# New orders of work for the first and last step of an attention loop, and two key tiles summed on TensorE

## The reference

```
x = x + attention0(layernorm(x))        # 16 heads of 64, no mask
    q, k, v = z @ wq @ fcq_w + fcq_b, ...          # per head
    attn    = softmax(q k^T / 8) over 1024 keys
    out     = (attn v) over all heads @ fco_w + fco_b
x = x + experts0(layernorm(x))          # 8 experts, top 2
x = x + attention1(layernorm(x))        # latent keys, rotary, causal
x = x + experts1(layernorm(x))          # 9 experts of width 512
```

## Time and profile before

| what | value |
|---|---|
| timed runs | 1471.29 us median (1468.84 to 1474.14) |
| profiled execution | 1475.02 us, span 1473.3 us |
| mean granted TensorE clock | 0.965 |
| busy over the span | PE 93%, DVE 66%, POOL 59%, ACT 55% |
| step 0 | 64.8 to 107.5 us |
| last step to the middle part | about 692 to 737.7 us |

### The profile page before, as it was taken

One profiled execution on the slowest core, in us unless ns is written; L12 is line 12 of the kernel. 1 busy time (PEld: TensorE's weight loads), 2 busy tenths in 40 slices (PEclk: granted clock), 3 DMA queues, 4 the chain that ended last, 5 costly groups with the idle time before them and its releaser, 6 DMA issues. The chain is left out here.

```text
span 1473.3 us, 18699 instructions
## 1 busy us (share of the span) xinstructions
PE 1367.5 (93%) x6354; PEld 791.1 (54%) x6354; DVE 974.1 (66%) x1675; ACT 810.0 (55%) x1236; POOL 870.9 (59%) x685
## 2 busy tenths in 40 slices
PE   7699999999999999999888876999999988999998
PEld 5345555455544555455366633454445446687776
DVE  5676767767776766666556568677666624566665
ACT  4234454454444454354354452566776666787776
POOL 0277888988888888878544405555655232344443
PEclk9699999999999999999999898999999997999999
DMA  3101111111101111000050006011111107000000
GB/s 107 33 1 59 59 59 59 44 59 59 46 28 59 58 59 45 1 16 27 15 160 1 1 1 100 16 30 30 30 22 24 30 1 273 1 1 8 8 8 8
DMA packets 32586, 60.59 MB, mean 41 GB/s; under 512 B 9499, under 2 KB 17084, under 8 KB 32348
## 3 DMA queue, kind: packets, MB, share of 16 engines
q1 hardware_dynamic: 32492, 59.40, 14.6%
HBM read 35.13 MB, written 13.89 MB: 33 GB/s over the span
## 5 line engine op out<-in xcount | busy, mean ns | idle before, releaser
L628 POOL TENSOR_TENSOR psum_k<-psum_k,prob 128x1024 f32<-128x1024 f32 x186 | 466.6, 2541 | 115.4 <-ACT prob L680 114.9
L680 ACT ACTIVATE prob<-pair 128x1024 f32<-128x1024 f32 x256 | 247.7, 1027 | 367.1 <-PE pair L934 366.9
L739 DVE TENSOR_REDUCE mx<-pair 128x2 f32<-128x1024 f32 x256 | 297.2, 1214 | 40.4 <-PE pair L865 38.5
L906 PE MATMUL pv<-prob,c_all 128*64 128x512 f32 x1024 | 251.0, 607 | 0.9 <-ACT plain L648 0.9
L1937 DVE CUSTOM_DVE_ANT_0 l_banks<-l_banks,causal 128x128 f32<-128x128 f32 (+7 forms) x256 | 189.4, 782 | 75.5 <-PE l_banks L1975 74.4
L1845 ACT ACTIVATE l_prob<-l_banks 128x1024 f32<-128x1024 f32 (+7 forms) x256 | 155.2, 654 | 111.7 <-PE l_banks L1994 111.1
L933 PE MATMUL pair<-qq,ak 128*128 128x512 f32 x512 | 210.9, 412 | 6.0 <-issue 2.8
L934 PE MATMUL pair<-q,kb 128*128 128x512 f32 x512 | 203.5, 397 | 0.0
L2153 POOL TENSOR_TENSOR silu_rest_t<-silu_t,silu_lead_t 128x512 fp32r<-128x512 f32 x74 | 96.3, 1303 | 145.9 <-ACT silu_lead_t L2350 145.9
L1899 POOL TENSOR_SCALAR_AFFINE_SELECT l_prob<-l_prob 128x128 f32<-128x128 f32 x256 | 72.3, 295 | 146.7 <-ACT l_prob L1845 145.1
L933 PEld LDWEIGHTS pair<-qq,ak 128*128 128x128 f32 x512 | 97.7, 191 | 70.4 <-issue 29.2
(11 more groups left out here) (318 smaller groups left out, 2283.0 us busy)
## 6 DMA issues: line engine op xcount, KB each, us to landing
plain<-scratch_sums SPq DMA_DIRECT2D x32, 256.0 KB
whole<-in_experts SPq DMA_DIRECT2D x12, 512.0 KB, 5.0
scratch_lead<-rounded SPq DMA_DIRECT2D x12, 512.0 KB, 2.6
scratch_rest<-rounded SPq DMA_DIRECT2D x12, 512.0 KB, 3.9
w_lead_t<-scratch_lead SPq DMA_DIRECT2D x9, 512.0 KB, 6.4
w_rest_t<-scratch_rest SPq DMA_DIRECT2D x9, 512.0 KB, 7.3
l_kk<-rounded SPq DMA_DIRECT2D x16, 256.0 KB, 4.2
l_qq<-rounded SPq DMA_DIRECT2D x16, 256.0 KB, 5.3
```

The costliest lines, as they stand in the source:

```text
L628: nc.gpsimd.tensor_tensor(total[:, h, :], total[:, h, :], prob[kt % 4][:, h, :], ALU.add).then_inc(summed, 1)
L680: nc.scalar.activation(prob[kt % 4][:, :, ts(j, BLK)], buffer("ST", at)[:, :, :], ACT.Exp, scale=D0 ** -0.5).then_inc(exp_done, 1)
L739: nc.vector.reduce_max(mx[:, x % 2, :, x // 2], buf[:, :, :], AX.X).then_inc(read, 1)
L906: ins = nc.tensor.matmul(pv[D0 * h:D0 * (h + 1), ts(j, BLK)], m.c_all[:, TT * (s // PAIRS) + kt, :], prob[kt % 4][:, h, ts(j, BLK)], start ...
```

## The change

It adds an order for step 0, changes the order of the last step, and takes key tiles 6 and 7 of the last step out of the adds on GpSimd and VectorE; TensorE takes their probabilities in as further parts of the last sums.

```
+FIRST_STEP = ("PV PV q q ST ST ST ST ST s s PV s s PV PV s s PV ST ST ST ST ST ST ST s PV s s s PV PV PV "
+              "s s s PV PV s s PV PV s s ST ST m ST ST PV PV ").split()
-LAST_STEP = ("ST ST ST ST PV PV PV PV ST ST ST ST l PV PV PV PV ST ST ST ST PV PV r PV PV ST ST ST ST n "
+LAST_STEP = ("ST ST ST ST PV PV PV PV ST ST ST ST l PV PV PV PV ST ST ST r ST PV PV n ST ST ST ST PV PV "
              "PV PV PV PV g ").split()
-TURN_AT, ROOT_AT, NORMAL_AT, LEAD_AT, EXP_AT = 6, 12, (4, 6), 12, 4
+TURN_AT, ROOT_AT, NORMAL_AT, LEAD_AT, EXP_AT = 6, 12, (4, 6), 12, 3
...
-    for kind in STEP if n + 1 < STEPS0 else LAST_STEP:
+    for kind in FIRST_STEP if n == 0 else STEP if n + 1 < STEPS0 else LAST_STEP:
...
+SUMMED_LAST = TT - 2
...
-                for kt in range(1, TT):
+                for kt in range(1, TT if n < LAST else SUMMED_LAST):
...
-                    add_last(rest[0])
+                    if rest[0] < SUMMED_LAST:
+                        add_last(rest[0])
...
-                    if rest[0] == 2:
+                    if rest[0] == TT - 1:
                         index_two(nc, m, link)
...
-                    await_sums(pe, k, TT - 1)
-                    for q in range(4):
-                        ins = nc.tensor.matmul(buf[32 * q:32 * (q + 1), 0, :], ones[:, 0:32],
-                                               psum_k[k % 2][:, q // 2, ts(q % 2, BLK)], start=True, stop=True)
+                    parts = [psum_k[k % 2]]
+                    if k == LAST:
+                        parts += [prob[kt % 4] for kt in range(SUMMED_LAST, TT)]
+                    await_sums(pe, k, SUMMED_LAST - 1 if k == LAST else TT - 1)
+                    for i, part in enumerate(parts):
+                        for q in range(4):
+                            ins = nc.tensor.matmul(buf[32 * q:32 * (q + 1), 0, :], ones[:, 0:32],
+                                                   part[:, q // 2, ts(q % 2, BLK)], start=(i == 0),
+                                                   stop=(i == len(parts) - 1))
```

## The result

The changed kernel takes 1462.57 us in the median of six runs (1460.2 to 1465.46), where the kernel before takes 1472.45 on the same chip (six runs, 1468.84 to 1475.48). The ratio is 0.9933 with a 95% interval of 0.9917 to 0.9950: about 9.9 us less (7.4 to 12.2). A second measurement of the same kernel, further down, gives 0.9942 (0.9924 to 0.9960). So the kernel is faster by 0.6 to 0.7%, where 11.2 us, 0.76%, was forecast. The profiled execution has a span of 1459.4, 13.9 under the 1473.3 of before.

The account below looks back on a forecast made before the run. TensorE was taken to set the pace, so time removed from its stream arrives at the end. Step 0's 6.6 us plus the last step's 4.7 less 0.1 gave 11.2: 1460.0 us timed, 8-in-10 range 1454.5 to 1467.

Parts of the forecast that it names:

- step 0: First loop step: its gains and losses from the new order were summed to 6.6 us gained.
- q units in front: Step 0 start: step 1's two q units fill the DMA wait; first scores 0.5 us later, 1.9 leave the later stream.
- Clock in step 0: Step 0, first scores: TensorE's clock rises earlier, near 67.8; 1.4 us gained, bounds 0 to 2.6.
- The cover of the q units: Step 0: ScalarE's and VectorE's work on q runs behind half-clock TensorE work; cost nothing, at most 1.7 us.
- The full ring behind seven score units: Step 0, middle: the ring of three tiles runs full, the third row-max unit waits for an exponential; 0.7 us lost.
- The wait at step 1: Step 0 end: more units behind the turned maxima cut the DMA wait from 1.79 to 0.3 us; 1.5 won.
- Clock in step 1: Step 1's first 16 score matmuls: full speed, 3.88 instead of 5.38 us; 1.5 gained, bounds 0 to 1.5.
- GpSimd passes it through: Start of step 1: GpSimd's lag is 6 us instead of 6.8, so step 0's gain passes at no cost.
- The last step: Last loop step: TensorE's waits go, extra sums are added; 4.7 us gained, less 0.1 for a delayed copy.
- The copy of step 14's sums: Last step: VectorE copies near 708.6 instead of 711.49, so TensorE's 1.06 us idle time goes.
- `on`: Last step: ready at 721.7, 2.3 us before TensorE's output product asks; 1.1 late if VectorE's add follows GpSimd's.
- The extra sums: Last step's end: three sets of last sums instead of one add 2.0 us, from 1.7 to 3.4.

Follow-up runs that it names:

- first_only: Changed kernel with its last step set back (old order, all adds on GpSimd and VectorE, search after the second add): 1465.92 us, ratio 0.9948.
- after_again: The changed kernel unedited, run once more as base for a comparison on one chip: 1462.49 us, ratio 0.9942.
- exp_early: Changed kernel with one extra one-column exponential on ScalarE ahead of the loop, so the table loads in idle time: 1461.43 us, ratio 0.9925.
- adds_back: Changed kernel with key tiles 6 and 7 of the last step again added by GpSimd and VectorE: 1461.28 us, ratio 0.9922.
- after: The changed kernel itself, in its first measurement and profile: 1462.57 us, ratio 0.9933.
- index_early: Changed kernel with the index search behind the second add of the last step again: 1463.71 us, ratio 0.9944.
- q_front: Changed kernel, but step 0 in the old order with only the two q units moved to the front: 1465.77 us, ratio 0.9942.
- m_sooner: Changed kernel, but step 0 in the old order with only the turn of the maxima moved ahead: 1469.37 us, ratio 0.9974.
- sums_only: Kernel before, old orders, with only the two extra parts in the last sums on TensorE: 1468.15 us, ratio 0.9970.
- last_only: Changed kernel with the old order in step 0, so only the last step is changed: 1469.53 us, ratio 0.9968.
- best: Changed kernel with all adds back on GpSimd and VectorE, index search behind the add of tile 5, and an early exponential: 1460.04 us, ratio 0.9927.

## Why the prediction was right

The mechanism held in both ends. For the last step the agreement is firm: 4.6 was forecast (4.7 less 0.1), and the traces with the old and the changed last step differ by 4.5 to 4.6 whichever two are taken. For step 0 the agreement to 0.1 is in part luck: several terms were off and balanced, and some of them change from one execution to the next.

- **q units in front.** Forecast: scores 0.5 later. They start 4.52 behind the turn instead of 3.83: 0.7; in `first_only`, where the clock rose earlier, 0.
- **Clock in step 0.** Forecast 1.4 of a bound of 2.6. All of 2.6 came in this execution: the granted clock is 1.00 from 65.00 on. The rise came 4.6 behind the turn here (60.44 to 65.0), not the 5.9 behind a start without a break that the prediction took. The term varies: with the same order the first four score matmuls were slow in `after_again` and `exp_early`, two in `adds_back`, and in `first_only` the clock rose during the q units. A rise within the first scores is also worth less than it looks, since `after`, `after_again`, `adds_back` and `index_early` all turn the next maxima at 36.27 to 36.28: what the clock gives there, the waits of the next point take.
- **The cover of the q units**, costed at nothing, was not whole. The first five score units take 5.9 (64.96 to 70.88) where 4.85 is full speed: TensorE waits 0.40 for VectorE's subtractions and 0.24 for the first exponential, together 1.1 between the starts. The second row-max unit, which was to lose nothing once q was done, comes another 0.4 late, behind an exponential. Of this 1.5, within the bound of 1.7, 0.9 is the table load, as `exp_early` shows; the other 0.6 is VectorE's subtractions, which come behind ScalarE's activations of the q units. The prediction had the half clock as their cover, and in this execution the scores ran at full clock. I had not asked where the first exponential's table load would go once four other activations stood in front of it.
- **The full ring behind seven score units**, forecast at 0.7, cost nothing: the third row-max unit behind the run starts 0.34 after the second.
- **The wait at step 1.** Forecast 0.3, measured 0.64. The work behind the turn takes 4.5 where 4.28 was summed, and the row came 5.15 behind the turn, where it had come after 4.54. That differs from one execution to the next: wherever TensorE waited for it in this case, it came 4.20 (`q_front`) to 5.15 behind the turn, and `after_again` and `index_early` show no wait at all. `m_sooner` and `q_front` show that the wait goes with the place of the turn, and that VectorE's row maxima must keep up.
- **Clock in step 1.** Forecast 1.5, measured 1.6 in this pair of traces. It is not a fixed gain: `q_front` waited 1.45 and `sums_only` 1.56 without falling, the kernel before 1.79 and `last_only` 1.91 with a fall (granted clock 0.53 and 0.58 behind it). An execution of the kernel before in which the clock does not fall has 1.6 less to give. That may be why the timed gain is 9.9 and 8.5 rather than 11.2. The scatter of 4 us behind the loop could do it as well; the timed runs carry no trace, so neither is shown.
- **GpSimd passes it through.** Right: GpSimd is 6.8 behind at the start of step 1, before and after, and from the q units of step 1 to the sums of step 14 every trace takes 591.6 to 592.2, before included.
- **The last step.** Forecast 4.6, measured 4.6. The copy of step 14's sums was expected 0.5 ahead of the scores of tile 4 and came 1.5 behind them, since both adds waited for GpSimd (6.75 for two); it cost 0.3 of waiting before the scores of tile 5. `on` had 3.4 to spare instead of 2.3. The extra sums cost 1.7, the lower bound, not 2.0. These two balanced.
- **What the prediction gave no share.** It counted order and sums as one, so it missed that either alone ends the wait for `on`, and that with the order in place the sums on TensorE cost 0.6 more than they bring (`adds_back`).

## What to carry over

Where one engine streams without a pause in the steady part of a loop, look at its first and last turn: work that needs no transfer belongs into the wait for the first one, and what releases the next turn belongs as far ahead as its own inputs allow. When two edits remove the same wait, try each alone, since the second can then be pure cost. When the order of activations changes, ask where the table load moves. And measure an edit on the shortest stretch that holds it: here the last step repeated to 0.04 us, while the timed intervals of most variants overlap.

## What the runs showed of the hardware

A short vector instruction can be held until GpSimd's add beside it ends. In `best` a product of 128x8 took 2.15 (L1038 above) while its twin at 713.16 took 0.16. In the kernel after, the gate product of 128x64 (L1018) took 1.92 at 693.60 and ended within 0.1 of GpSimd's add (692.07 for 3.36); in the kernel before it took 0.23 at 703.53, with GpSimd idle. The Trainium skill (GPSIMD Engine Reference, 1. Specifications) names this contention, for vector instructions of two inputs in SBUF among others, without its cost, and the runs agree with it. A cast with one input was held too: 128x16 took 1.17 at 709.58 in `best`, beside GpSimd, and 0.18 at 714.91 in the kernel after, with GpSimd idle. Not every short one is held: of the five from that cast to the twin, two were, and the others took 0.16 to 0.20. In the kernel after, VectorE's add started 0.04 ahead of GpSimd's and had its full speed (1.23 at 705.12), and GpSimd's two took 6.76.
